# Vision tower block with a mixture of experts: routing and expert tiles in one phase, or in two

## What is computed

```
h = state_space_kernel(x)                      # (8, 256, 512)
h = concat([cls_tok, h], axis=1)               # (8, 257, 512)
h = h + attention(layernorm(h))                # 16 heads of 32
y = layernorm(h)
probs = softmax(y @ router_w + router_b)       # 8 experts
top_p, top_i = top_k(probs, 2); top_p /= sum(top_p)
out_e = gelu(y @ expert_w[e] + expert_b[e])    # for the two chosen
h = h + (sum of top_p * out_e) @ out_w + out_b
```

## Time and profile before

| | us |
|---|---|
| median of 3 runs | 741.27 (740.93 to 743.52) |
| profiled execution, first to last instruction | 742.2 |
| of this, PE busy | 677.8 |
| DVE busy | 525.4 |
| ACT busy | 412.8 |
| POOL busy | 152.6 |

### The profile page before, as it was taken

How to read it: one execution, slowest core, us unless ns; L and a number is a source line. 1 busy time by engine, 2 the same in 40 slices (tenths; PEclk the granted TensorE clock), 3 DMA queues, 4 the chain that set the end, 5 groups by cost and what they waited for, 6 DMA issues and landing times.

```text
span 742.2 us, 16679 instructions
## 1 busy us (share of the span) xinstructions
PE 677.8 (91%) x5671; PEld 541.1 (73%) x5672; DVE 525.4 (71%) x1210; ACT 412.8 (56%) x1073; POOL 152.6 (21%) x306
## 2 busy tenths in 40 slices
PE   4788977889999999999999999889679999998998
PEld 3577867767778787777878777656347888886886
DVE  7999883655788777787877877677884444445775
ACT  5864544486767677676766666665723333333111
POOL 5200001010121111201112020113132223336650
PEclk9889999979999999999999999999789999999999
DMA  7501255300000010000100003216626765556895
GB/s 202 198 1 29 115 143 145 73 1 1 3 29 30 0 56 0 29 28 14 42 0 28 28 28 115 85 58 227 256 60 207 206 202 162 167 168 204 263 325 172
DMA packets 54553, 76.11 MB, mean 103 GB/s; under 512 B 24666, under 2 KB 26970, under 8 KB 54387
## 3 DMA queue, kind: packets, MB, share of 16 engines
q1 hardware_dynamic: 40850, 42.43, 17.7%
q0 software_dynamic: 5920, 19.40, 9.9%
q10 hardware_dynamic: 7744, 13.77, 5.0%
HBM read 45.42 MB, written 30.16 MB: 102 GB/s over the span
## 4 chain that ended last, share of the span: by engine, by line
PE 72%; DVE 17%; ACT 4%; issue 3%; DMA 2%; POOL 1%; ACTq 0%; DVEq 0%; POOLq 0%; SPq 0%
PE ps L1978 45%; PE ps L2084 8%; PE ps L2094 4%; PE ps L2077 4%; PE ps L2145 3%; DVE ring L1409 3%; DVE ring L1408 3%; PE ps L1925 2%; PE ps L2101 1%; ACT prb L1029 1%; PE ps L1956 1%; ACT pts L1037 1%; DVE ew_lo L1720 1%; PE ps L1969 1%; PE ps L2044 1%
## 5 line engine op out<-in xcount | busy, mean ns | idle before, releaser
L1037 ACT ACTIVATE pts<-ps 128x512 f32<-128x512 f32 x128 | 77.0, 602 | 98.2 <-PE ps L2084 98.1
L1029 ACT ACTIVATE prb<-ps,negmax 128x257 f32<-128x257 f32 x256 | 117.7, 478 | 5.2 <-DVE negmax L1479 4.3
L1479 DVE TENSOR_REDUCE negmax<-ps 128x2 f32<-128x514 f32 x128 | 82.5, 686 | 22.4 <-PE ps L2077 22.4
L2084 PE MATMUL ps<-ident,prb 128*128 128x128 f32 x512 | 84.0, 287 | 5.7 <-ACT pts L1037 3.2
L2084 PEld LDWEIGHTS ps<-ident,prb 128*128 128x128 f32 x512 | 57.1, 143 | 30.8 <-issue 13.1
L1488 DVE TENSOR_SCALAR prb<-prb,rrec 128x258 f32<-128x258 f32 x256 | 73.5, 351 | 2.3
L1211 ACT ACTIVATE rows<-ps 128x512 f32<-128x512 f32 x40 | 23.9, 598 | 87.5 <-DVE ps L1835 85.5
L1978 PE MATMUL ps<-ew_hi,xnT_hi 128*128 x160 | 66.7, 417 | 3.0 <-DVE xnT_lo L1756 2.4
L1978 PE MATMUL ps<-ew_lo,xnT_hi 128*128 x160 | 63.5, 397 | 0.0
L1978 PE MATMUL ps<-ew_hi,xnT_lo 128*128 x160 | 63.0, 394 | 0.0
L839 POOL DMA_INDIRECT rows<-xn_dram,token_of x40 | 39.6, 990 | 106.9 <-PE ps L2145 87.1
(11 more groups left out here) (402 smaller groups left out, 1761.1 us busy)
## 6 DMA issues: line engine op xcount, KB each, us to landing
y_slots<-rows ACTq DMA_DIRECT2D x40, 256.0 KB
ew<-in_L_ffn_expert_w_dram SPq DMA_DIRECT2D x8, 1024.0 KB, 9.1
h_dram<-h_ob SPq DMA_DIRECT2D x17, 256.0 KB, 2.0
xn_dram<-tok SPq DMA_DIRECT2D x17, 256.0 KB, 2.2
h_late<-h_dram SPq DMA_DIRECT2D x12, 256.0 KB
out_dram<-h_late SPq DMA_DIRECT2D x11, 256.0 KB
y_slots<-u_sb SPq DMA_DIRECT2D x9, 256.0 KB, 5.4
tok_dram<-so SPq DMA_DIRECT2D x4, 512.0 KB, 3.1
```

Source lines behind the costliest of these rows:

```text
L1029: e = act.activation(prb[:, u % 2, j, 0:KEYS], ps[:, j, 0:KEYS], ACT.Exp, bias=negmax[:, u % 2, j:j + 1], accum_out=rowsum[:, u % 2, j:j + 1])
L1037: act.activation(pts[:, slot:slot + 2, :, st * P:(st + 1) * P], ps[:, 4, :].rearrange("p (h t s) -> p h t s", h=2, t=HALVES), ACT.Copy).th ...
L1479: dve.tensor_reduce(negmax[:, u % 2, 2 * b:2 * b + 2], ps[:, 2 * b:2 * b + 2, 0:KEYS], AX_X, ALU.max, negate=True).then_inc(s["dve_max"], 1)
L2084: mm = pe.transpose(ps[:, 4, (2 * j + tt) * P:(2 * j + tt + 1) * P], prb[:, u % 2, 2 * b + j, tt * P:(tt + 1) * P], ident[:, :])
```

## The change

Only the last batch and what follows it are changed in their order; the buffers in SBUF are laid out anew for it.

- The three quads of batches 0 to 5 (12 token tiles, `EARLY_TILES`) are routed inside the last batch, in a program written out for each engine (`last_batch`). `turn_xn` uses banks 7 and 5 in turn, DVE keeps the even tiles and ACT the odd ones. The projection of batch 6 moves behind the turns of unit 7, and all of `pv` of the last batch behind unit 7.
- Whatever the routing is, 12 x 128 tokens with two choices each fill at least 16 whole tiles (`FULL`). A first table for these is made behind the last batch (24 columns instead of 34, 16 tiles instead of 40), with `token_of[:, 0:16]` and `expert_of[:, 0:16]`.
- The first two tiles run, then the last five token tiles are turned; the third tile waits for all low parts; logits of the last two quads stand behind tile 2, their sums behind tile 3, the ranks behind tile 5, and the second table's 34 matmuls behind tile 12. DVE makes the rest of the routing in eleven pieces behind the biases of tiles 3 to 14, ACT the gates' exponential behind tile 7 and its half of the second table behind tile 9.
- DVE makes all low parts of the experts' weights; `expert_rest` and `keep_expert_low` are gone.
- SP loads experts 0, 1, 4, 3, 2 during the last batch, 5, 6 and the biases behind `pv`, 7 behind the class projection. `ow` and the early tiles of `h` are loaded from tile 16 on.

```diff
-    SPLITS = (0, 8, 16, 24)
-    LOWS_IN_ATTENTION = 3
-    EARLY_QUADS = 2
+    EARLY = NB - 2
+    FULL = (SEL * EARLY * BODY - NE * (P - 1)) // P
+    REST = SLOTS - FULL
+    ACOLS = EARLY * HALVES * SEL
+    PAIRS = [NB // 2 - 2] + list(range(NB // 2 - 2)) + [NB // 2 - 1]
+    EARLY_QUADS = EARLY // 2
...
 # SP
+            sp.wait_ge(s["pe_pv"], NB * KC)
+            sp.wait_ge(s["dve_key_probs"], 2 * NB)
+            for e in range(5, 7):
+                load_expert(e)
+            sp.dma_start(eb[:, :, :]...).then_inc(s["loaded_biases"], 16)
+            for st in range(HALVES):
+                keep_h(last, st)
+            sp.wait_ge(s["pe_cls_projected"], 1)
+            load_expert(NE - 1)
...
 # POOL
+            pool.wait_ge(s["dve_token_of"], 1)
+            for i in range(2):
+                gather(i)
+            for st in range(HALVES):
+                last_bias(last, st)
             norm_pow(last)
+            for i in range(2, 4):
+                gather(i)
...
+            for i in range(4, FULL):
+                gather(i)
+            pool.wait_ge(s["dve_token_of"], 2)
+            for i in range(FULL, SLOTS):
+                gather(i)
...
 # ACT
+            for i in range(2, FULL):
+                if i > 2:
+                    hi_xs(i + 1, i + 1, False)
+                store_slots(i - 1, i - 1)
+                gelu(i, i, False)
+                if i == 7:
+                    act.wait_ge(s["dve_gate_gap"], 1)
+                    act.activation(spread[:, 1, :], spread[:, 0, :], ACT.Exp)
+                if i == 9:
+                    act.wait_ge(s["dve_hit"], 2)
+                    act.activation(of_tile_b[:, :, 1, :], hit_b[:, :, :], ACT.Copy, scale=part[:, 0:1])
...
 # DVE, behind the first token_of
+            for st in range(HALVES):
+                residual(last, st, 6 + st)
+                residual_stats(last, st)
+            for st in range(HALVES):
+                normalise(last - 1, st)
+            lo_xs(0, 0)
+            norm_sums(last)
+            lo_expert(1)
+            lo_xs(1, 1)
...
+            for st in range(HALVES):
+                normalise(last, st)
+            lo_expert(2)
+            lo_expert(3)
...
+            for e in range(4, NE):
+                lo_expert(e)
+            lo_xs(2, 0)
+            add_bias(0, 0)
+            lo_xs(3, 1)
+            add_bias(1, 1)
+            rest = {3: rest_logits, 4: rest_count, 6: rest_tiles, 7: rest_of_first, 8: rest_of_last, 9: rest_hit,
+                    10: rest_tile_table, 11: rest_place_table, 12: rest_experts, 13: rest_token_of, 14: rest_gates}
+            for i in range(2, FULL):
+                if i > 2:
+                    lo_xs(i + 1, i + 1)
+                add_bias(i, i)
+                if i in rest:
+                    rest[i]()
...
 # PE, unit 7 of the last batch and on
+                open_unit(7)
+                first_turns(7)
+                logits_of(2)
+                second_turns(7)
+                project(c - 1, 0, 7)
+                sum_chunks(2)
+                project(c - 1, 1, 6)
+                first_turns(8)
+                pv(c, 0, 0)
+                second_turns(8)
+                rank(cum_a, 1, 5)
+                for gr in range(1, KC):
+                    pv(c, gr, gr)
+                key_turn(c, 4)
+                pe.wait_ge(s["dve_key_probs"], 2 * NB)
+                project(c, 0, 6)
+                project(c, 1, 7)
...
+            turn_xs(0, 0)
+            turn_xs(1, 1)
+            expert(0, 0, True)
+            turn_xs(2, 0)
+            expert(1, 1, True)
+            for n in range(EARLY_TILES, NT):
+                turn_xn(n)
+            turn_xs(3, 1)
+            pe.wait_ge(s["dve_expert_low"], NE)
+            expert(2, 0, False)
+            for q in range(EARLY_QUADS, len(QUADS)):
+                logits_of(q)
+            turn_xs(4, 0)
+            expert(3, 1, False)
+            for q in range(EARLY_QUADS, len(QUADS)):
+                sum_chunks(q)
+            for i in range(4, FULL):
+                turn_xs(i + 1, i + 1)
+                expert(i, i, False)
+                if i == 5:
+                    rank(cum_b, 2, 2)
+                if i == 12:
+                    rest_table()
```

More of the change, by code:

```diff
@@ L392, in vit_tower_kernel @@
             "dve_hit": "the slots' tiles, one-hot",
-            "dve_onehot": "the slots' tiles times the tokens' tiles, then pieces of the slots' places, one-hot",
+            "dve_onehot": "the slots' tiles times the tokens' tiles, then the slots' places, one-hot",
+            "dve_places": "the slots of the first tokens, their places among them",
             "dve_token_of": "the token of every slot",
@@ L1103, in body @@
                     if u == 2:
[L1104 to L1106 removed]
+                        exp_cls(c)
                         keep_v(c, 1)
@@ L1111, in body @@
                         value_low()
-                    if u == 3 and not last:
+                    if u == 3:
                         act.wait_ge(s["pe_values"], (c + 1) * HALVES)
@@ L1685, in _, with rounded, running_sums @@
+            def rounded(out, src, add, by):
+                then(dve.tensor_scalar(out, src, add, by, ALU.add, ALU.mult))
+                then(dve.tensor_scalar(out, out, ROUND_MAGIC, ROUND_MAGIC, ALU.add, ALU.subtract))
+            def running_sums(sums, order):
+                for (i, o), level in zip(zip(order, order[1:]), (1, 2, 4)):
+                    then(dve.tensor_tensor(sums[:, o, 4:], sums[:, i, 4:], sums[:, i, 4 - level:4 - level + NE], ALU.add))
             for m in range(KC):
@@ new lines, in _ @@
+            dve.scalar_tensor_tensor(out=place_a[:, :], in0=tile_a[:, :], scalar=-float(P), in1=slot_a[:, :],
+                                     op0=ALU.mult, op1=ALU.add).then_inc(s["dve_places"], 1)
+            tck_copy(last, 4)
+            cells = [P, ACOLS, FULL]
+            dve.tensor_tensor(hit_a[:, :, :], bc(iota_slot[:, 0:FULL].unsqueeze(1), cells),
+                              bc(tile_a[:, :].unsqueeze(2), cells), ALU.is_equal).then_inc(s["dve_hit"], 1)
+            dve.wait_ge(s["dve_places"], 1)
@@ new lines, in lo_xs @@
+            def lo_xs(i, u):
+                dve.wait_ge(s["act_slotT_high"], i + 1)
+                lo_turned(4 + u % 2, u % 2, "dve_slotT_low")
+            cells = [P, SLOTS, NE]
+            then(dve.tensor_tensor(reached_a[:, :, :], bc(iota_i[:, :].unsqueeze(2), cells),
+                                   bc(full_to[:, 1, 4:].unsqueeze(1), cells), ALU.is_ge))
+            then(dve.tensor_reduce(tile_expert[:, 0, :], reached_a[:, :, 0:NE - 1], AX_X, ALU.add))
+            then(dve.scalar_tensor_tensor(out=tile_expert[:, 0, :], in0=reached_a[:, :, NE - 1], scalar=1.0 - NE,
+                                          in1=tile_expert[:, 0, :], op0=ALU.mult, op1=ALU.add))
@@ new lines, in _ @@
+            dve.tensor_copy(expert_of[:, 0:FULL], tile_expert[:, 0, 0:FULL]).then_inc(s["dve_expert_of"], 1)
+            lo_expert(0)
+            dve.wait_ge(s["stored_xn"], 16 * EARLY_TILES)
+            dve.wait_ge(s["pe_token_of"], 1)
+            then(dve.tensor_copy(token_tile[:, 0:FULL], ps[:, 5, 2 * NE:2 * NE + FULL]))
+            dve.scalar_tensor_tensor(out=token_of[:, 0:FULL], in0=token_tile[:, 0:FULL], scalar=float(P),
+                                     in1=ps[:, 5, 2 * NE + FULL:2 * NE + 2 * FULL], op0=ALU.mult, op1=ALU.add
+                                     ).then_inc(s["dve_token_of"], 1)
@@ L1737, in _ @@
-            for st in range(HALVES):
-                normalise(last, st)
+            lo_expert(1)
+            lo_xs(1, 1)
             dve.wait_ge(s["loaded_cls"], 16)
@@ L1748, in _ @@
                               ).then_inc(s["dve_stats2"], 1)
-            lo_expert(1)
+            for st in range(HALVES):
+                normalise(last, st)
+            lo_expert(2)
+            lo_expert(3)
             dve.wait_ge(s["pool_rstd"], NB + 1)
@@ L2261, in body @@
                         turn_p(pc, pu, 1)
-                    if u in (3, 4) and last:
-                        turn_xn(2 * u - 5)
                     if u == 0 and not first:
```

1224 lines of the change are left out of this document (708 added, 516 removed).

## The result

The changed kernel took 751.1 us in the median of four runs (747.6 to 752.9), the kernel before 741.1 us beside it: a ratio of 1.0117, 95% interval 1.0095 to 1.0139. So it is slower, by 7.0 to 10.3 us. Forecast were 746.5, which is 5.2 more, in a range of 740 to 752.

The account below looks back on a forecast made before the run. PE was taken to bound the expert tiles, DVE the routing stretch ahead of them. Early gain -5.0, PE work +5.2, slow tile +1.8 and stalls +3.2 gave +5.2 us on 741.27: 746.5, range 740 to 752.

Parts of the forecast that it names:

- a doubled gather: First gather behind token_of, slowed by expert loads: +4.2 us instead of +1.0, total 749.7; chance 0.1.
- The last batch neither gains nor loses: Last attention batch: third quad's logits reach DVE at 501.1 us, where the second quad's were taken at 501.6 before.
- DVE's segment, 23.4 us: DVE's work from the third quad's logits at 501.1 sums to 23.4 us, so token_of stands at 524.5.
- The gather, 4.2 + 1.0: First gather, token_of to first turned row: 4.2 us as before, plus 1.0 for expert loads in flight.
- From lo_xs(0) to the third tile, 21.25: DVE's pieces from lo_xs(0) at 531.0 sum to 21.25 us, so the third tile starts at 552.4.
- The third tile 5.0 earlier: Early phase: third expert tile starts at 552.4 instead of 557.4, the early phase's whole gain of 5.0 us.
- What lies between the tiles, 10.2: From the third tile on: 10.2 us laid behind its start, from PE's work 5.2, slow tile 1.8, stalls 3.2.
- PE's own work between tiles, 5.2: Late logits, sums, ranks and the second table's 34 matmuls (1.9) cost PE 5.2 us between the tiles.
- The slow tile, 1.8: Third tile runs at the lower clock behind PE's idle time from 545 to 552.4, costing 1.8 us.
- Stalls, 3.2: PE's waits between tiles: 0.45 at slot 7 (Exp's table), 0.7 at slot 9, 2.1 at gather(16); together 3.2 us.
- Table switches at 2.6 us: ACT's switches for Exp and Gelu between tiles cost 2.6 us each, not 1.28; total 748.5, chance 0.15.
- The faster case: DVE's pieces fill gaps in the last batch; third tile before 543.5; at 541 the total is 735.1; chance 0.15.

Follow-up runs that it names:

- best_xn: best_load with ACT's copy of the fourth turned tile moved ahead of unit 4's four exponentials in the last batch; 739.3 us, ratio 0.9963.
- before_dve_lows: The kernel before with one part of the change alone: DVE makes all eight experts' low halves, PE and ACT none; 744.9 us, ratio 1.0031.
- own_low: Changed kernel, but each full tile waits only for its own expert's low half, experts 4 to 7 made behind tiles 2, 5, 9, 13; 752.9 us.
- warm: Changed kernel with 22 extra unread matmuls in PE's idle time, 12 behind the second tile and 10 behind turn_xs(3); 752.1 us, ratio 1.0126.
- token_swap: Changed kernel with DVE's second token_of moved behind tile 12's bias, ahead of the second list of experts; 750.4 us, ratio 1.0102.
- exp_late: Changed kernel with ACT's exponential of the gates behind the last Gelu and DVE's three gate instructions behind the last bias; 754.6 us, ratio 1.0174.
- gathers_first: Changed kernel with POOL's third and fourth gather ahead of the last batch's two bias additions and its power; 751.5 us, ratio 1.0136.
- best: Changed kernel with a low-half gate per tile, gathers_first, token_swap, and an 8 column Gelu ahead of the late copies; 749.3 us, ratio 1.0079.
- best_load: best with SyncE's load of expert 7's matrix issued ahead of the two stores of h; 744.2 us, ratio 1.0018.
- key_token: Changed kernel with DVE's class key copy ahead of the slot computation and token_of ahead of the first low half; 751.5 us, ratio 1.0128.
- best_key: best_load with key_token's two moves on DVE as well; 743.9 us, ratio 1.0017.
- pool_idle: Changed kernel with POOL's four output bias additions in the last two batches cut from 512 columns to 8; median 753.8 us, ratio 1.0131.

## Why the prediction came out as it did

The sign and the range held; the sum was 4.4 us short by the profile (+9.6 where I had +5.2), and 3.6 of this are in one term, the start of the third tile. That 751.1 lies inside 740 to 752 is in part luck. The top of the range was there for a drain beside the table loads and for a doubled gather, neither of which came; other things filled it.

- *The last batch neither gains nor loses.* This step failed. The third quad's logits reach DVE at 497.76, or 503.5 on the clock of before, not at 501.1. I had counted the wait for ACT's copy, but not that PE behind such pauses runs at half clock: logits_of(0) took 1.94 us and logits_of(1) 1.61 instead of 1.06, and the turns and scores behind them took 1.45, 0.95 and 1.06 in the chain instead of 1.0, 0.56 and 0.59. That is 2.7 us and more than covers the 2.4. And I took that wait as given, where best_xn shows that it was worth 2.9 us.
- *DVE's segment, 23.4 us.* Measured 23.1 (497.76 to 520.85). Right, though token_of was released through PE's half-clock projections (4.93) and lo_expert(0).
- *The gather, 4.2 + 1.0.* It took 4.1 us from token_of's end at 520.85 to PE's turn at 524.98, with the loads in flight: in this trace my 1.0 was 0. In nine other profiles with the same order it took 4.0 to 5.1, so some of the 1.0 does occur. The case of a doubled gather is out. Turn and high part took the 1.3 that I had (524.98 to 526.24); lo_xs(0) came 0.65 later, at 526.89, because DVE was still at the slow pair of 3.56 us.
- *From lo_xs(0) to the third tile, 21.25.* Measured 23.3 (526.89 to 550.21). The low halves of experts 2 and 3 took 5.54 us as a pair instead of 4.4. And I had left out the end of the chain: the bias, Gelu(0) and its release, 1.5 us between DVE's last low part and PE. (531.0 and 21.25 are 552.25; the prediction has 552.4.)
- *The third tile 5.0 earlier.* With these, 1.4. Late logits 2.4, this stretch 2.1, less 0.3 for the segment and 0.5 for the way to lo_xs(0), make the 3.6 up to rounding. DVE as the gate is shown by before_dve_lows, and by own_low for the first 2.9 us.
- *What lies between the tiles, 10.2.* Measured 11.0, but by two errors that cancel: PE's own work was 1.8 less, the stalls 2.4 more.
- *PE's own work between tiles, 5.2.* 3.4: logits 1.21, sums 1.01, ranks 0.35, the table's 34 matmuls 0.87 where I had 1.9. Those ran in 0.026 us each; my 0.053 came from a row of ten that had just begun behind a wait, and with 80 columns instead of 48. Which of the two makes the difference no run shows.
- *The slow tile, 1.8.* 2.0 (4.75 against 2.73), shown by warm.
- *Stalls, 3.2.* 5.6 (what is left of 11.0). By steps between tiles over 3.2 us: behind the ranks 0.4, at the ninth tile 1.6, at the eleventh 1.3, behind the table 0.2, at the 16th 2.4. (They add up to 5.9; the kernel before has one such step, too, 4.0 from the fourth to the fifth tile.) The last was forecast at 2.1 and token_swap takes it away. The ninth was 0.45: Exp's loads are 0.7 of it, and 0.9 stay in exp_late, where PE waits for DVE; I had taken DVE's first-slot pieces to hide in 2.1 us. The eleventh was 0.7. A reason that these stalls share stands below.
- *Table switches at 2.6 us.* Out: Exp starts 0.01 us behind its load's end and the load 0.02 behind the Gelu. The Trainium skill's drain of 1.38 us beside the load (ScalarE: Activation LUTs, What ACT_TABLE_LOAD costs) doesn't show here; its 1.28 for the load does.
- *The faster case* had its condition in the third tile before 543.5 on the clock of before. best_xn brings it to 544.2 (542.82, and 1.39 for the turns of unit 3, at 473.49 there and at 469.12 + 5.76 in the changed kernel). From there to the last tile it has 9.5 us more than the kernel before (128.2 against 118.7), so by the profile it is 3.7 us faster, by the ratio 0.7 to 4.7.

The stalls come out longer for one reason, as an estimate. I gave a tile's low part 1.0 us to spare (559.61 against 557.36 + 3.2). In PE's order of time, before, the next tile's first matmul is here:

```profile
560.29 0.48 PE L1978 MATMUL ps<-ew_hi,xnT_hi 128*128 x1
```

A PE that waits starts 0.14 us behind the low part's end (586.76 and 586.90 after). That leaves 0.5 to spare, and the stalls at the ninth and the eleventh tile are longer by as much.

One thing that the prediction doesn't have at all is that DVE's low halves and POOL hold each other up. In the changed kernel the low halves of experts 2 and 3 take 5.54 us beside POOL's addition to the class row, 2.76 us long there. In gathers_first, best and best_xn the addition has ended when they begin: they take 4.47 us, it 1.26 to 1.28.

What stays open: how much of the 4.1 us between best_load and best_xn is the clock's luck (each has one profile), and what a clean test of token_of's chain would give, with lo_expert(0) neither ahead of token_of nor beside the gather.

## What to carry to other kernels

Work moved ahead of a phase gains only as far as the last wait ahead of that phase, so write that wait's whole chain out, up to the matmul (here low part, bias, Gelu and its table), and look for the second and third wait behind it: the second was 3 us away here. Work laid into a dense loop of one engine costs its length there, and a stall wherever the other engines' own slack is already spent by another piece. When an instruction is moved on one engine, follow its semaphore to the queues that wait for it (POOL's addition held SyncE's stores, these the next load), and look at what it will then run beside (DVE's low part held POOL's gather in own_low, key_token and best_key). Try the cheap swaps of order first: one line on ACT, into a 0.9 us gap, was worth more than the early gathers.

## What the runs showed of the hardware

- Kernels that are the same up to there ran the same 12 matmuls at 4.33 or 2.79 us (batch 0, before and after), the same eight logits at 1.94 or 1.07 us behind pauses of 2.89 and 2.88 us (after and best_load), and the same 16th tile at 3.02 or 4.61 us behind pauses of 1.73 and 1.76 us (after and warm). So the length of a pause alone doesn't say whether the lower clock follows, and runs of one kernel spread by 3 to 11 us.
- DVE and POOL held each other up. POOL instructions that began while a low part ran on DVE ended only behind it, and the next low part then waited for POOL's: the second of two took 3.35 us instead of 2.28 (pool_idle). POOL's addition of 128x512 took 1.28 us (best), 2.76 (after, begun 0.64 us behind the first of two low parts) or 5.44 (best_load, begun 0.17 us behind the first, and ended behind both). POOL's power of two columns took 0.70 us, or 2.70 when begun 0.16 us behind a low part. Two DVE instructions of 128x512 took 3.56 us beside two POOL additions of 2.52 together, and 0.99 without them.
- The issue of a gather on POOL is held up in the same way: 0.95 or 1.25 us, but 2.75 (own_low) and 3.01 (key_token, best_key) when a low part on DVE had begun 0.4 us earlier.
- Table matmuls (128x48, bf16) run at 0.026 us each when 34 follow one another, and so did the 24 of 32 columns in the first table (0.62 us).
